# The Newton step and the scaling of a decoder's layer norms on GpSimd in place of VectorE

## The reference

```python
x = _ln(x + self_attention(x))              # 16 heads of 8, rotary embedding
x = _ln(x + cross_attention(x, context))    # 16 heads, biases
x = _ln(x + mixture(x))                     # 8 experts 128-512-128, relu, softmax weights of the top 2
x = _ln(x + causal_attention(x))            # one head, scores x qk x^T / sqrt(128)
x = _ln(x + cross_attention(x, context))    # 16 heads, no biases but the last
x = _ln(x + routed_mixture(x))              # one expert per token, capacity 128 per expert
```

## Time and profile before

| | us |
|---|---|
| median of 3 runs | 437.92 |
| lowest and highest | 437.26, 438.38 |
| the profiled execution | 437.39 |
| its span | 435.6 |
| TensorE busy | 370.9 |
| VectorE busy | 282.0 |
| ScalarE busy | 226.1 |
| GpSimd busy | 53.8 |

### The profile page before, as it was taken

One profiled execution on the slowest core, in us unless ns is written; L12 is line 12 of the kernel. 1 busy time (PEld: TensorE's weight loads), 2 busy tenths in 40 slices (PEclk: granted clock), 3 DMA queues, 4 the chain that ended last, 5 costly groups with the idle time before them and its releaser, 6 DMA issues.

```text
span 435.6 us, 8944 instructions
## 1 busy us (share of the span) xinstructions
PE 370.9 (85%) x3188; PEld 324.7 (75%) x3188; DVE 282.0 (65%) x833; ACT 226.1 (52%) x526; POOL 53.8 (12%) x61
## 2 busy tenths in 40 slices
PE   4478899999889999999968999899999789863492
PEld 3367777777779997989967999788997577632491
DVE  6388898888965557632795455844866887825353
ACT  2126476575666564766347555684557455711231
POOL 6600002920000000000000000000002002010125
PEclk9999999999999999999989999999999989975598
DMA  4547511113440000200020000200011115700301
GB/s 129 159 115 247 140 36 44 47 37 108 130 113 34 2 2 2 73 2 2 2 72 2 2 0 2 74 2 1 2 47 41 42 32 159 239 15 0 109 13 33
DMA packets 22459, 25.14 MB, mean 58 GB/s; under 512 B 3208, under 2 KB 17169, under 8 KB 22416
## 3 DMA queue, kind: packets, MB, share of 16 engines
q1 hardware_dynamic: 21184, 23.14, 18.1%
q0 software_dynamic: 512, 0.97, 0.7%
q10 hardware_dynamic: 720, 0.46, 0.3%
HBM read 17.82 MB, written 6.83 MB: 57 GB/s over the span
## 4 chain that ended last, share of the span: by engine, by line
PE 68%; DVE 17%; issue 7%; ACT 3%; DMA 2%; SPq 1%; POOL 0%; POOLq 0%; DVEq 0%; ACTq 0%
PE bank_D L847 13%; PE bank_C L737 10%; PE bank_D L711 8%; PE bank_A L722 7%; DVE negmax L1214 5%; PE bank_A L863 4%; PE bank_A L865 3%; PE bank_A L864 3%; PE bank_D L637 2%; PE bank_D L695 2%; PE bank_D L767 1%; PE bank_A L777 1%; DVE q_sp L1209 1%; PE bank_A L1518 1%; PE bank_D L750 1%
## 5 line engine op out<-in xcount | busy, mean ns | idle before, releaser
L1214 DVE TENSOR_REDUCE negmax<-bank_D 128x2 f32<-128x512 f32 x192 | 127.5, 686 | 43.0 <-PE bank_D L711 42.9
L986 ACT ACTIVATE expo<-bank_A 128x512 f32<-128x512 f32 x192 | 110.1, 597 | 53.3 <-PE bank_A L722 51.9
L711 PE MATMUL bank_D<-k_head,q_sp 128*128 128x256 f32 x384 | 90.3, 320 | 11.2 <-DVE negmax L1214 5.1
L722 PE MATMUL bank_A<-q_sp,k_head 128*128 128x256 f32 x384 | 82.0, 298 | 4.9 <-DVE q_sp L1209 3.4
L1022 ACT ACTIVATE hidden<-bank_A,b 128x256 f32<-128x256 f32 x128 | 53.7, 471 | 52.1 <-PE bank_A L865 52.0
L711 PEld LDWEIGHTS bank_D<-k_head,q_sp 128*128 128x128 f32 x384 | 61.0, 197 | 23.5 <-issue 13.0
L847 PE MATMUL bank_D<-mix_w,hidden 128*128 128x128 f32 x512 | 67.8, 275 | 0.0
L722 PEld LDWEIGHTS bank_A<-q_sp,k_head 128*128 128x128 f32 x384 | 60.0, 192 | 7.9 <-DVE q_sp L1209 5.3
L847 PEld LDWEIGHTS bank_D<-mix_w,hidden 128*128 128x128 f32 x512 | 62.5, 191 | 1.6 <-issue 1.6
L737 PE MATMUL bank_C<-expo,v_aug 128*32 128x256 f32 x768 | 48.0, 392 | 2.0 <-ACT expo L986 1.9
L1273 DVE SCALAR_TENSOR_TENSOR y_mixture<-bank_D,g_w,y_mixture 128x128 f32<-128x128 f32 x64 | 22.3, 349 | 30.5 <-PE bank_D L847 28.8
(11 more groups left out here) (174 smaller groups left out, 511.1 us busy)
## 6 DMA issues: line engine op xcount, KB each, us to landing
mix_w<-in_mix_w SPq DMA_DIRECT2D x24, 256.0 KB, 3.9
k_head<-k_scratch SPq DMA_DIRECT2D x96, 48.0 KB
k_scratch<-qk_hi SPq DMA_DIRECT2D x24, 128.0 KB, 2.3
w_last<-in_mix_w SPq DMA_DIRECT2D x8, 256.0 KB, 5.5
k_scratch<-qk_lo SPq DMA_DIRECT2D x12, 128.0 KB, 2.4
proj_w<-in_proj SPq DMA_DIRECT2D x1, 640.0 KB, 6.5
xe_scratch<-empty_row SPq DMA_DIRECT2D x1, 520.0 KB, 4.5
expo<-xe_scratch SPq DMA_DIRECT2D x2, 260.0 KB, 3.3
```

Of the source, the lines that this page charges most:

```text
L711: last = mm(where(seq, b, ("max", k))[:, qt * SEQ:(qt + 1) * SEQ], q_sps[SET[seq, b]][:, k // 4, qt * P:(qt + 1) * P], k_heads[SET[seq, b] ...
L722: last = mm(where(seq, b, ("exp", h))[:, kt * SEQ:(kt + 1) * SEQ], k_heads[SET[seq, b]][:, t, g, kt * P:(kt + 1) * P], q_sps[SET[seq, b]][ ...
L986: activate(expo[:, exp_slot(seq, b, h), :], where(seq, b, ("exp", h))[:], ACT.Exp, scale=float(HD) ** -0.5).then_inc(free(seq, b, ("exp", ...
L1214: V.tensor_reduce(negmaxes[SET[seq, b]][:, s // 4, :, 32 * (s % 4)], where(seq, b, ("max", s))[:].rearrange("p (q n) -> p q n", q=QT), AX. ...
```

## The change

`normalise` is taken from VectorE's program and put into GpSimd's, where it is called at the turn "xT" of each sequence and block, the turn in which TensorE transposes that x. VectorE's three Newton instructions, of two operations each on two tensors, become five on GpSimd: add eps, times r, times r, times -0.5 plus 1.5, times r. Each raises `norm_own` and is waited for. The two scalings are the same instruction as before, on GpSimd. Moments and first guess stay where they are.

Since VectorE no longer writes x itself, waits are added: before the sum that overwrites y (attention and causal) for the x of the program before, before the scatter for its sequence's x, and before the last stage's norm for all four.

```diff
+                def normalise(seq, b):
+
+                    pool.wait_ge(rstd0_ready[seq], b + 1)
+                    r, (n0, n1, n2) = r0[b][:], (newton[b][:, i, :] for i in range(3))
+                    G = nc.gpsimd
+                    link(G.tensor_scalar(n0, mv[b][:, :, 1], EPS, None, ALU.add))
+                    link(G.tensor_tensor(n0, n0, r, ALU.mult))
+                    link(G.tensor_tensor(n1, n0, r, ALU.mult))
+                    link(G.tensor_scalar(n1, n1, -0.5, 1.5, ALU.mult, ALU.add))
+                    link(G.tensor_tensor(n2, n1, r, ALU.mult))
+                    for qt in range(QT):
+                        last = G.tensor_scalar(x[seq][:, qt, :], y[b][:, qt, :],
+                                               mv[b][:, qt, 0:1], newton[b][:, 2, qt:qt + 1],
+                                               ALU.subtract, ALU.mult)
+                    last.then_inc(x_ready[seq], 1)
...
                     pool.wait_ge(slot_ready, seq + 1)
+                    pool.wait_ge(x_ready[seq], CROSS1 + 1)
...
                         residual(seq, b, residuals[b])
+                    elif what == "xT":
+                        normalise(seq, b)
...
-                def normalise(seq, b):
-
-                    dve.wait_ge(rstd0_ready[seq], b + 1)
-                    r, (n0, n1, n2) = r0[b][:], (newton[b][:, i, :] for i in range(3))
-                    link(V.scalar_tensor_tensor(n0, mv[b][:, :, 1], const[:, C_EPS:C_EPS + 1], r,
-                                                ALU.add, ALU.mult))
-                    link(V.scalar_tensor_tensor(n1, n0, -0.5, r, ALU.mult, ALU.mult))
-                    link(V.scalar_tensor_tensor(n2, n1, 1.5, r, ALU.add, ALU.mult))
...
                             dve.wait_ge(xb_ready[seq], MHA[b] + 1)
+                            if (seq, b) in NEXT_TO:
+                                earlier, block_before = NEXT_TO[seq, b]
+                                dve.wait_ge(x_ready[earlier], block_before + 1)
...
                             wait_filled(dve, seq, b, "out")
+                            if seq:
+                                dve.wait_ge(x_ready[seq - 1], b + 1)
...
+        for normalised in t["x_ready"]:
+            dve.wait_ge(normalised, CROSS1 + 1)
         layernorm(0, x_rows, x_norm, x_norm_ready)
```

More of the change, by code:

```diff
@@ L405, in decoder @@
         slot_ready = sem("slot_ready")
-        pool_own = sem("pool_own")
+        pool_own, norm_own = sem("pool_own"), sem("norm_own")
         w1_split = sem("w1_split")
@@ L500, in decoder @@
             drained=drained, xe=expo, xeT=xT_all, x_norm=cT_all, ye=v_augs[1], ye_norm=v_augs[0],
-            hid=hidden, ident=ident, scattered=scattered, w1_loaded=w1_loaded, w2_loaded=w2_loaded))
+            hid=hidden, ident=ident, scattered=scattered, w1_loaded=w1_loaded, w2_loaded=w2_loaded, x_ready=x_ready))
         with nc.Block() as block:
@@ L514, in residual, with link @@
                     ).then_inc(xb_ready[seq], 1)
+                own = [0]
+                def link(instruction):
+                    own[0] += 1
+                    instruction.then_inc(norm_own, 1)
+                    pool.wait_ge(norm_own, own[0])
+                def normalise(seq, b):
[12 more added lines that the diff above has]
+                    last.then_inc(x_ready[seq], 1)
                 def split_weights(e):
@@ L1201, in attention @@
                             moments(seq, b)
-                        if s == NORM_AT:
-                            normalise(seq, b)
                         if group_at(s, SHIFT_AT) is not None:
@@ L1280, in mixture @@
                             moments(seq, b)
-                        if s == MIX_NORM_AT:
-                            normalise(seq, b)
                         yield
@@ L1311, in causal @@
                             moments(seq, b)
-                        if s == CAUSAL_NORM_AT:
-                            normalise(seq, b)
                         yield
```

## The result

| | median us | lowest to highest |
|---|---|---|
| before | 437.73 | 437.26 to 438.38 |
| changed | 448.73 | 448.06 to 449.76 |

The ratio is 1.0248 (interval 1.0222 to 1.0273): slower, by 11.0 us, where 436.1 us was forecast. The profiled execution of the changed kernel took 448.31 us, its span is 446.5 us against 435.6.

What follows compares the result with a forecast made beforehand. TensorE, busy 370.9 of 435.6 us, was taken as the bound, so only its waits for x counted: -0.87 - 1.00 - 1.13 + 0.78 + 0.36 = -1.86 us on the 437.92 median, 436.1 us, range 433.8 to 440.3.

Steps and rivals of the forecast that it cites:

- Added on GpSimd: Cost of each norm on GpSimd: five small chained instructions at 0.20 us and two scalings at 0.30, together 1.6 us.
- T: Length of one norm on GpSimd: forecast 1.6 us, ends 1.36 and 2.23, where VectorE needs 1.25.
- rival of more relief: VectorE's freed time also helps in its full stretches: 5.6 us more, 430.5 us; chance 0.12, shared with a clock staying up.
- its own rule: Between 1.6 and 2.23, each 0.1 us of T costs 0.8 in all: 0.1 at A, C, D, F, 0.2 at B, E.
- A: Second norm, slowed on VectorE while GpSimd splits weights: x comes earlier on GpSimd, gain 0.87 us.
- B: First place with two norms together, which VectorE reaches late: second transposition starts earlier, gain 1.00 us.
- C: The mixture's third norm: x just in time for TensorE, no gain or loss, but no reserve.
- D: The mixture's fourth norm, behind two indirect DMAs and the residual in GpSimd's queue: loss 0.78 us.
- E: Second place with two norms together: first x without a wait, second transposition earlier, gain 1.13 us.
- F: Last norm, which nothing hides, so TensorE waits for all of it: loss 0.36 us.
- At the twelve nothing: At 12 of 20 norms TensorE is still at other work when x is ready: no gain or loss counted.
- Slower, because the norm on GpSimd is long: Rival: from T = 1.99 us the kernel is slower by over 1.31 us; T = 2.5 gives 443.3; chance 0.21.

Runs made afterwards that it cites:

- probe: Kernel before plus fourteen single GpSimd instructions, each waiting for the one before, mostly on 128x128 float32, where GpSimd is idle: 438.51 us in one execution.
- no_newton: Changed kernel without the five Newton instructions, GpSimd scaling with the first guess: 434.33 us, ratio 0.9931 to the kernel before.
- eight_on_pool: Changed kernel with only the eight norms of over 3.2 us reserve on GpSimd, the other twelve on VectorE: 438.06 us, ratio 0.9983.
- both: Like pairs_split, and GpSimd's split of the mixture's weights also waits until the second norm is done: 434.52 us, ratio 0.9949 to the kernel before.
- no_newton_dve: Kernel before without its three Newton instructions, all norms staying on VectorE: 432.35 us, ratio 0.9898.
- pairs_split: Changed kernel with all norms on VectorE except the first of each of two adjacent pairs, done by GpSimd: 435.92 us, ratio 0.9966 to the kernel before.
- scale_on_dve: Changed kernel with the two scalings back on VectorE, the Newton step staying on GpSimd: 440.85 us, ratio 1.0074 to the kernel before.

## Why the prediction was wrong

**The step that failed is "Added on GpSimd".** It put T at 1.6 us with an upper end of 2.23, and T is 3.03. Both terms were too small:

- a small step is 0.29 us instead of 0.20; five are 1.45 instead of 1.0. The upper end, 0.29, had it. The value was taken nearer to a MEMSET of one column, 0.103, but an instruction that computes on two columns is 0.19 to 0.23 long;
- a scaling is 0.797 us instead of 0.30; two are 1.58 instead of 0.6. No end held this: the upper one was the two-input instruction, 0.39. The probe shows that this estimate was good for its own form, and that two per-partition columns cost twice as much. The bound was set by the number of tensors read, where the kind and number of the scalars decide.

With that the range was too narrow for its own terms, too: it ended at 440.3, below the 441.1 that it gives for T = 2.23 and the 443.3 for T = 2.5 (and its lower end, 433.8, lay above the 430.5 of its rival of more relief). Its ends are also 0.1 and 0.2 us off its own rule (434.9 - 1.0 = 433.9; T = 2.1 gives 440.1).

**The places and the rule between T and time held.** Lateness is how much later TensorE starts a transposition than in the trace of before. The last column is how much it grows from the last transposition of the norm ahead to the last of the place. Beside it stands the prediction's own rule with T = 3.03 (its value at each place, and 1.43 us on top, twice at B and E):

| place | forecast, T = 1.6 | its rule, T = 3.03 | measured |
|---|---|---|---|
| A | -0.87 | +0.56 | +0.59 |
| B | -1.00 | +1.86 | +1.99 |
| C | 0 | +1.44 | +1.02 |
| D | +0.78 | +2.21 | +2.33 |
| E | -1.13 | +1.73 | +1.56 |
| F | +0.36 | +1.79 | +1.64 |
| norms 1, 3, 4 | 0 | 0 | +0.32 each |
| norm 19 | 0 | 0 | +0.84 |
| sum | -1.86 | +9.6 | +10.9 |

The six places alone sum to 9.1 measured and 9.6 by the rule. The rest of the span's +10.9 us balances out: +0.86 ahead of the first norm and +0.80 behind B, against -0.77 behind C, where TensorE had waited 0.65 us for ScalarE before and doesn't now, and -0.95 behind the last norm. So the rule's 437.73 + 9.6 = 447.3 us, 1.4 below the measured 448.73, is as near partly by luck: four norms that it doesn't hold make +1.8 of their own.

no_newton is the check at the other end: its waits for x came as forecast, 1.79 us less against 1.86, and its time, 434.33 where 436.1 was forecast, was lower still.

**"At the twelve nothing" held for T = 1.6, not for this one.** At norms 1, 3 and 4 the transposition comes 2.9 us after the Exp, which with the prediction's 0.05 and 0.10 leaves room for a T of 2.75. VectorE's 1.25 us fits, and so does 1.6; 3.03 doesn't, and TensorE waits 0.15 or 0.16 at each. Norm 19 has 2.50 us before, room for a T of 2.35, and waits 0.66 now; it would have been exposed at the rival's T of 2.5 already. The prediction counted how many norms have a wait, and not how large each reserve is; for a T that is an estimate, the second is what bounds the error.

**The relief of VectorE was worth nothing that shows**, as forecast. From 60 to 80 us it went from 17.83 us busy to 15.14, and TensorE did not get denser:

```profile
60.00:80.00 20.00, 17.84 (x166) 14.31 (x166) 15.14 (x32) 12.77 (x27) 5.54 (x12) 1.00 0.15 40
```

From the first norm on, TensorE's waits other than those for x stayed within 0.05 us, for example 0.79 and 1.53 for VectorE's reduces and 0.46 for q; the two exceptions are 0.09 us more ahead of C and the 0.65 less behind it. The forecast of VectorE's saving was high, 25 to 28 us against 21.0: 1.25 us is the stretch from the first start to the last end, and it holds the gaps between the steps and an overlap with the next instruction, 0.2 us in all.

**The rival that came true** was "Slower, because the norm on GpSimd is long", given 0.21. Its T of 2.5 was still short. The sentence beside it, the Trainium skill's rule (GPSIMD Engine Reference, Key points) that VectorE is about twice as fast in elementwise work, was nearer than the rows chosen: 3.03 against 1.25 is 2.4. The argument against it, that the CAST row didn't bear it out, compared an instruction without scalars.

**The clock** moved as the earlier trace rows had hinted, against the change. These rows run from the second transposition of B to the next norm's, the same TensorE work in each, with no wait for x inside. They give busy us (instructions) by engine, granted clock, DMA share and GB/s, for the kernel before, the changed one, eight_on_pool, both and no_newton_dve in this order:

```profile
223.00:255.36 32.36, 31.02 (x252) 28.74 (x253) 18.94 (x55) 20.76 (x51) 0.00 (x0) 0.95 0.06 18
227.44:260.60 33.16, 31.87 (x252) 29.46 (x253) 17.27 (x48) 20.73 (x51) 3.12 (x8) 0.92 0.05 13
223.44:256.61 33.17, 31.91 (x251) 29.50 (x252) 18.37 (x50) 20.76 (x51) 2.60 (x7) 0.92 0.06 18
222.07:253.24 31.17, 29.39 (x254) 27.10 (x253) 18.41 (x55) 21.01 (x52) 0.30 (x1) 1.00 0.09 25
220.94:252.18 31.24, 29.46 (x252) 27.18 (x252) 18.18 (x52) 21.27 (x53) 0.00 (x0) 1.00 0.10 27
```

The changed kernel takes 0.80 us longer than the one before, at a mean clock of 0.92 against 0.95. That it is the clock and not the norm is seen in eight_on_pool: there VectorE still does both norms of B, and at the same 0.92 the stretch is as long. Where the clock stays at 1.00 the stretch is 1.1 to 1.2 us shorter than before. So the microsecond that the prediction priced for a clock that stays up does exist, but not in the kernel that it was priced for. In the changed kernel TensorE was busy only 1.55 of 4 us ahead of and around that transposition, and then the whole 4 us at 0.50, the lower level of 1.2 GHz:

```profile
224.00:228.00 4.00, 1.55 (x7) 0.96 (x7) 0.68 (x1) 0.98 (x2) 3.45 (x9) 0.50 0.41 112
228.00:232.00 4.00, 4.00 (x19) 3.82 (x19) 2.66 (x8) 1.91 (x5) 0.00 (x0) 0.50 0.31 85
```

What decides whether the clock falls at B isn't shown: both and pairs_split wait the same there (0.47 and 0.48 us), and behind it the clock is 1.00 in one and 0.95 in the other.

## What to carry to other kernels

Before work is moved to a slower engine, list for each place how long after the input the consumer really starts, and compare that reserve with the new latency; busy time that is freed elsewhere doesn't pay for it. A price for an instruction form that the trace doesn't show is not bounded by its neighbours, and a few microseconds of that form in an idle stretch of the kernel settle it. Where two such tasks came together here, one on each engine beat both on VectorE (pairs_split, 0.34%).

## What the runs showed of the hardware

- GpSimd's `tensor_scalar` on 128x128 float32 is priced by its scalars (probe): 0.54 to 0.58 us with one plain number, 0.30 to 0.39 with two, 0.60 with one per-partition column, 0.80 with two. `tensor_tensor` with a broadcast column is 0.40, and 0.61 for 128x256. That one number costs more than two was not expected, and it is not explained here. By these numbers a scaling of both tiles by two `tensor_tensor` instructions of 128x256 would be about 1.2 us instead of 1.58, an estimate that was not run.
- A chain of small instructions on GpSimd goes at 0.29 us a step (the changed kernel, 1.45 us for five), one on VectorE at 0.21.
- Two scalings on VectorE beside GpSimd's split take 1.75 us or 1.95 (scale_on_dve), alone 0.61; beside GpSimd's scalings only 0.60 to 0.75. How much GpSimd holds VectorE up differs by what GpSimd does.
- The same stretch of TensorE work, behind B, takes 31.2 us at a mean granted clock of 1.00, 32.4 at 0.95 and 33.2 at 0.92.
